# Picking a looked-up row by its high digit: a chain of conditional copies, or one masked product and one sum

## The chip, the cores and the metric

The kernel runs on one core of a Trainium2 chip. The metric is the device time of one execution in microseconds, the median over runs; the profile is of one execution.

## What is computed

A layer of a graph network: 12,500 nodes with 16 features, 400,000 edges with 64 attributes each and a weight; edges are sorted by destination.

```python
h = max(layernorm(x), 0)
h = h @ W_node.T                       # 12500 x 16
rf = edge_attr @ W_review.T            # 400000 x 16
m = (h[src] + rf) * edge_weight
out = x + segment_sum(m, dst, 12500)
```

The products with the weights are made after the sums: attributes and rows of h are summed by destination first, and the 96-row sum is multiplied by both weights at the end.

## The kernel before

**Two ways to fetch h[src].** The edges are cut into 25 blocks of 125 lists of 128 edges. For 10 blocks ("gathered") GpSimd fetches the rows of h by indirect DMA, 1250 transfers of 128 rows (L487), with 8 slots of 5 transfers in flight; it waits for the slot to be summed (summed_p). For the other 15 blocks ("sorted") the sources of each list were sorted at the start, so rank j of each of the 125 lists points near row 98 x j of the table. TensorE looks the rows up by a product with a 0/1 matrix.

**The lookup.** The table of h lies in SBUF as fp16 in two parts (top and rest), 98 chunks of 128 rows. A source is split in a low part (one of 512, the "hot" matrix, 4 columns of 128) and a high digit of up to 8 values. A list block is worked in STEPS = 16 steps of RANKS = 8 ranks. In a step, `look_up` (TensorE, 64 matmuls, L969) makes for each of the 8 ranks a product with WIDTH[x] candidates of 16 features, one for each value of the high digit, into PSUM tile found[x % 2]: 125 partitions (lists) x 8 ranks x WIDTH x 16. WIDTH is 4, 6, 7, 7, 7, 8 seven times, 7, 7, 6, 5: 112 in all. Then `choose` (VectorE) keeps the candidate of the right digit, in found_h[125, 128 ranks, 16]. The mask (uint8, one plane of 128 ranks per digit) is made once a list block by `mark` (L727).

**choose.** The first digit is a product found x mask (L737). Each further digit is a copy_predicated over the same 8 x 16 elements (L742), which waits for the semaphore `chosen` of the one before it. TensorE waits for the last one before it writes the same found again two steps later (L961), and before it turns found_h for the rest (turn_ranks, L974 to L977).

**The order of VectorE's work** is written out by hand. In step x of block u: choose(x - 1); two hot columns for a later step (make_hot, L702, 2004 fp16 each); add_step(x - 1), the adds of the previous sums into acc, each with a register load of its base from base_row (L763, L771) and a wait for the add before it (L767, L775); the 0/1 matrices that bring the rows of the block before back in the order of the edges (make_perm, L757); the hits of later groups (L746), for which ScalarE waits (L545). After step 15: choose(15), adds, then split_ranks (L784) after TensorE and ScalarE. TensorE in a step: look_up, unsort of the block before (L983), sums (L995, L1004). SP loads attributes and the rows of low parts. After 15 such blocks there is a last stretch of 16 steps without lookup, then the product with the weights and the output.

All of it runs in a loop over passes, of which this input needs one.

Of the kernel before, what the change touches and what calls it, by code (L numbers as in the profile page):

```python
# [13 lines left out]
P = 128  # L14
# [35 lines left out]
BEFORE = [sum(WIDTH[:x]) for x in range(STEPS + 1)]  # L50
ALL_WIDTHS = BEFORE[STEPS]

# [33 lines left out]
def bass_gnn_preln(  # L86
# [47 lines left out]
    with ExitStack() as ctx:  # L134
# [6 lines left out]
        acc = sb("acc", [FS, N + WINDOW])  # L141
# [12 lines left out]
        big = sb("big", [P, 2 * NA * HOT // 2 + P * H])  # L154
        hot = big[:, 0:NA * HOT].bitcast(F16).rearrange("p (k a n) -> p k a n", k=2, a=NA)
# [42 lines left out]
        back_row = sel_p[:, 0, 2:4, :].rearrange("p j w -> p (j w)")  # L198
        stat = sel_p[0:C, 1:3].rearrange("p s j w -> p (s j w)")[:, 0:4 * NP].rearrange("p (k i) -> p k i", k=4)
# [6 lines left out]
        start_row = sb("start_row", [P, P])  # L206
        top_row = sb("top_row", [P, P])
        limit = sb("limit", [P, P])
# [7 lines left out]
        base_row = sb("base_row", [1, NG], I32)  # L216
# [55 lines left out]
        found_in = sem("found_in")  # L272
        chosen = sem("chosen")
# [178 lines left out]
        def _(pool):  # L452
# [20 lines left out]
            nc.gpsimd.memset(acc[:], 0.0).then_inc(acc_step, 1)  # L473
# [125 lines left out]
        def _(dve):  # L599
# [60 lines left out]
            link(nc.vector.tensor_scalar(start_row[:], iota[:], 98.0 / 128.0, 49.0 / 128.0, ALU.mult, ALU.add))  # L660
            link(nc.vector.tensor_tensor(start_row[:], start_row[:], back_row, ALU.subtract))
            link(nc.vector.tensor_scalar(start_row[:], start_row[:], 0.0, 1.0 / 256.0 - 0.5, ALU.max, ALU.add))
            link(nc.vector.tensor_scalar(start_row[:], start_row[:], ROUNDER, None, ALU.add))
            link(nc.vector.tensor_scalar(start_row[:], start_row[:], ROUNDER, None, ALU.subtract))
            link(nc.vector.tensor_scalar(top_row[:], width_row[:], float(-NA), float(CHUNKS), ALU.mult, ALU.add))
            link(nc.vector.tensor_tensor(start_row[:], start_row[:], top_row[:], ALU.min))
            link(nc.vector.tensor_scalar(start_row[:], start_row[:], float(P), None, ALU.mult))

            dve.wait_ge(span_in, 16)
            nc.vector.tensor_copy(base_row[:], span_row[:, 0, :])  # L670
# [27 lines left out]
            nc.vector.tensor_scalar(limit[:], width_row[:], 2.0, None, ALU.subtract)  # L698
# [12 lines left out]
            with dve.Fori(0, end) as ps:  # L711
# [18 lines left out]
                def choose(u, x):  # L730
                    before = ps * (SORTED * ALL_WIDTHS) + u * ALL_WIDTHS + BEFORE[x]
                    dve.wait_ge(found_in, ps * (SORTED * STEPS) + u * STEPS + (x + 1))
                    if x == 0:
                        dve.wait_ge(mask_in, ps * SORTED + u + 1)
                    ranks = slice(x * RANKS, (x + 1) * RANKS)
                    of_digit = found[x % 2][0:C, :].rearrange("p (j b f) -> p b j f", j=RANKS, f=H)
                    nc.vector.tensor_tensor(found_h[:, ranks, :], of_digit[:, 0], mask[:, 0, ranks].unsqueeze(2).to_broadcast([C, RANKS, H]),  # L737
                                            ALU.mult).then_inc(chosen, 1)
                    for b in range(1, WIDTH[x]):
                        dve.wait_ge(chosen, before + b)  # L740
                        dve.sem_inc(begun_dve, 1)
                        nc.vector.copy_predicated(found_h[:, ranks, :], mask[:, b, ranks].unsqueeze(2).to_broadcast([C, RANKS, H]),  # L742
                                                  of_digit[:, b]).then_inc(chosen, 1)
# [51 lines left out]
                for step in range(STEPS):  # L795
                    if step:
                        choose(0, step - 1)
                    make_hot(0, step)
                    if step:
                        add_p(step - 1, step - 1, added + (step - 1))  # L800
# [288 lines left out]
```

## Time and profile before

| what | value |
|---|---|
| median of 3 runs | 2129.21 us (2125.23 to 2130.02) |
| profiled execution, time | 2126.73 us |
| profiled execution, span | 2124.9 us |
| mean granted TensorE clock | 0.863 of full |
| TensorE, VectorE, ScalarE, GpSimd busy | 78%, 74%, 42%, 68% |

The time includes what lies around the span from first to last instruction. Busy time is the union of an engine's instructions. "Idle before" is an engine's idle time just before a group of instructions, and behind the arrow what ended it; an idle time shorter than a certain size is counted but has no releaser named.

### The profile page before, as it was taken

The numbers are of one execution on the slowest core, as the hardware profiler recorded it, in microseconds if no ns is written. First come the engines' busy times: TensorE is split into PE (matmuls) and PEld (weight loads), VectorE is DVE, ScalarE is ACT, GpSimd is POOL, SyncE is SP. The second block draws the span as 40 slices with busy tenths as digits, with TensorE's granted clock in tenths as the row PEclk, the third lists the DMA queues.
The fourth block names the chain that finished last, engine by engine and source line by source line (L and its number), as shares of the span: only waits on it lengthen the run. The fifth ranks groups of instructions, "written<-read, shape, count | busy, mean of one in ns | idle before, by whom it ended". The sixth has DMA issues, their size and how long they took to land.

```text
span 2124.9 us, 75085 instructions
## 1 busy us (share of the span) xinstructions
PE 1650.7 (78%) x23874; PEld 1615.4 (76%) x23874; DVE 1575.2 (74%) x3975; ACT 895.3 (42%) x3561; POOL 1451.5 (68%) x1301
## 2 busy tenths in 40 slices
PE   1119887898878988887888879798887898878776
PEld 0018787888878888787888878788787888878765
DVE  5978777777777777777777777777777777777754
ACT  1212444444444444444544444444444444444452
POOL 2716777777767767676776767767676777767720
PEclk9559899988989899899988989889899989989855
DMA  3513344344444444444443444534444544434532
GB/s 116 80 39 88 75 98 104 81 98 98 87 98 94 96 99 86 97 99 86 98 93 84 102 89 86 114 80 86 105 90 87 103 88 97 99 80 106 100 52 44
DMA packets 512172, 191.43 MB, mean 90 GB/s; under 512 B 472234, under 2 KB 495359, under 8 KB 511479
## 3 DMA queue, kind: packets, MB, share of 16 engines
q1 hardware_dynamic: 469361, 173.64, 35.8%
q0 software_dynamic: 40000, 10.32, 5.0%
q8 instruction: 223, 3.65, 0.7%
q10 hardware_dynamic: 2368, 2.02, 0.4%
q14 instruction: 220, 1.80, 0.3%
HBM read 182.96 MB, written 2.89 MB: 87 GB/s over the span
## 4 chain that ended last, share of the span: by engine, by line
DVE 39%; issue 21%; DVEq 17%; PE 15%; ACT 4%; DMA 2%; SPq 1%; ACTq 1%
DVE big L742 15%; DVEq L771 7%; PE found L969 6%; DVE mid L746 5%; PE seg L1004 5%; DVEq L763 4%; DVE hit_p L746 4%; DVE perm L757 3%; ACT mid L545 3%; DVE big L702 2%; DVE big L737 2%; PE found L977 2%; DVE acc L775 1%; DMA w_rows<-in_L_gnn_W_node_dram 1%; PE seg L995 1%
## 5 line engine op out<-in xcount | busy, mean ns | idle before, releaser
L487 POOL DMA_INDIRECT vals_p<-h_ext,idx_t x1250 | 1436.5, 1149 | 586.2 <-issue 356.6
L969 PE MATMUL found<-table,big 128*128 128x128 f16 (+4 forms) x15360 | 891.5, 225 | 70.7 <-DVE by_rank L784 21.9
L969 PEld LDWEIGHTS found<-table,big 128*128 128x128 f16 x15360 | 871.4, 106 | 80.5 <-issue 79.9
L545 ACT ACTIVATE sel_p<-hit_p,wgt_t 128x64 f32<-128x64 f16 x1250 | 325.6, 336 | 1024.8 <-DVE hit_p L746 1022.4
L742 DVE COPY_PREDICATED big<-mask,found 125x128 f32<-125x128 uint8 x1440 | 434.3, 302 | 218.0 <-DVE big L742 15.6
L1004 PE MATMUL seg<-mid 128*96 128x64 f32 x3750 | 426.4, 277 | 210.6 <-ACT mid L558 210.4
L1004 PEld LDWEIGHTS seg<-mid 128*96 128x96 f32 x3750 | 401.4, 191 | 224.4 <-ACT mid L545 139.9
L545 ACT ACTIVATE mid<-mid,wgt_t 128x64 f32<-128x64 f16 x1875 | 467.9, 332 | 14.5 <-DVE mid L746 14.5
L702 DVE TENSOR_SCALAR big<-low_all,own 128x2004 f16<-128x2004 f16 x484 | 340.9, 747 | 11.9 <-DMA low_all<-low_dram 11.9
L775 DVE SCALAR_TENSOR_TENSOR acc<-seg,count_s,acc 96x64 f32 x375 | 105.0, 280 | 217.7 <-DVE acc L767 82.9
L995 PE MATMUL seg<-sel_p,vals_p 128*80 128x64 f32 x2500 | 235.2, 244 | 0.0
L995 PEld LDWEIGHTS seg<-sel_p,vals_p 128*80 128x80 f32 x2500 | 213.9, 160 | 0.1
L757 DVE TENSOR_TENSOR perm<-edge_no,pos_t 128x768 f16<-128x768 f16 x375 | 192.9, 546 | 0.0
L746 DVE TENSOR_TENSOR mid<-iota,rel_t 128x320 f16<-128x320 f32 x375 | 168.3, 480 | 0.0
L983 PE MATMUL edge_h<-by_rank,perm 128*128 128x32 f16 x1875 | 154.5, 241 | 8.1 <-DVE perm L757 5.6
L983 PEld LDWEIGHTS edge_h<-by_rank,perm 128*128 128x128 f16 x1875 | 126.4, 127 | 9.1 <-DVE perm L757 5.8
L746 DVE TENSOR_TENSOR hit_p<-iota,rel_t 128x320 f16<-128x320 f32 x250 | 119.8, 480 | 0.0
L767 DVE SCALAR_TENSOR_TENSOR acc<-seg,count_p,acc 80x64 f32 x250 | 68.2, 273 | 33.2 <-issue 31.6
L558 ACT COPY mid<-edge_h 128x160 f32<-128x160 f32 x375 | 88.7, 276 | 0.0
L977 PE MATMUL found<-ident,big 125*128 125x125 f32 x240 | 48.3, 386 | 49.8 <-DVE big L742 49.8
L977 PEld LDWEIGHTS found<-ident,big 125*128 125x128 f32 x240 | 43.9, 219 | 51.8 <-DVE big L742 51.8
L737 DVE TENSOR_TENSOR big<-found,mask 125x128 f32<-125x128 f32 x240 | 67.0, 279 | 0.2 <-PE found L969 0.2
(128 smaller groups left out, 316.1 us busy)
## 6 DMA issues: line engine op xcount, KB each, us to landing
low_all<-low_dram SPq DMA_DIRECT2D x120, 501.0 KB
mid<-in_edge_attr_dram SPq DMA_DIRECT2D x375, 160.0 KB
vals_p<-in_edge_attr_dram SPq DMA_DIRECT2D x250, 160.0 KB
vals_p<-h_ext,idx_t POOLq DMA_INDIRECT x1250
big<-in_src_dram SPq DMA_DIRECT2D x1, 1562.5 KB
big<-in_dst_dram SPq DMA_DIRECT2D x1, 1562.5 KB
big<-in_edge_weight_dram SPq DMA_DIRECT2D x1, 1562.5 KB
h_ext<-mid SPq DMA_DIRECT2D x2, 781.2 KB
```

The lines of the kernel that those rows point to most:

```text
L487: pool.indirect_dma_start(vals_p[:, q % RP, j, R:F], None, h_ext, bass.IndirectOffsetOnAxis(ap=idx_t[:, q * J + j:q * J + j + 1], axis=0), ...
L545: last = nc.scalar.activation(sel[:, j, :], hit[:, j, :], ACT.Copy, scale=wgt_t[:, bass.ds(tile + j, 1)])
L702: return nc.vector.tensor_scalar(hot[:, k, a, :], low_all[:, k, :], own[:, a:a + 1], None, ALU.is_equal)
L742: nc.vector.copy_predicated(found_h[:, ranks, :], mask[:, b, ranks].unsqueeze(2).to_broadcast([C, RANKS, H]), of_digit[:, b]).then_inc(cho ...
L746: return nc.vector.tensor_tensor(hit, iota[:, 0:WINDOW].unsqueeze(1).to_broadcast([P, J, WINDOW]), rel_t[:, bass.ds(tile, J)].unsqueeze(2) ...
L757: nc.vector.tensor_tensor(perm[:, g % RS], edge_no[:], pos_t[:, bass.ds(u, 1), g, :].to_broadcast([P, P, J + 1]), ALU.is_equal).then_inc(p ...
L771: base = dve.value_load(base_row[0:1, bass.ds(u * GROUPS + (NQ + g), 1)], min_val=0, max_val=N)
L969: last = nc.tensor.matmul(found[x % 2][:, r * P:r * P + n], hot[:, x // 2 % 2, a, col:col + P], rows, start=(a == 0 and part == 0), stop=( ...
L977: last = nc.tensor.transpose(found[i][:, f * P:f * P + C], found_h[:, :, i * HALF_F + f], ident[0:C, 0:C])
L983: last = nc.tensor.matmul(edge_of(g)[:, q * 2 * H:(q + 1) * 2 * H], perm[:, g % RS, :, q], by_rank[:, :, :, g * J + q].rearrange("p i f -> ...
L995: last = nc.tensor.matmul(seg_p(x), vals_p[:, slot, j, :], sel_p[:, x % RH, j, :], start=(j == 0), stop=(j == J - 1))
L1004: last = nc.tensor.matmul(seg_s(g), vals_s[:, g % RS, j, :], sel_s[:, g % RS, j, :], start=(j == 0), stop=(j == J - 1))
```

## The change

`choose` becomes two functions. `mask_found` multiplies all WIDTH[x] candidates of the 8 ranks with their masks in one instruction, into a new SBUF tile `masked` (125 x 8 x 8 x 16, fp32); `add_digits` sums over the digit with one tensor_reduce whose input is the view with the digit as inner axis, 16 elements apart. make_hot comes between the two. The semaphore `chosen` counts reductions, a new one `masked_in` counts products, and TensorE's look_up waits for `masked_in`.

```diff
-                def choose(u, x):
-                    before = ps * (SORTED * ALL_WIDTHS) + u * ALL_WIDTHS + BEFORE[x]
-                    dve.wait_ge(found_in, ps * (SORTED * STEPS) + u * STEPS + (x + 1))
+                def mask_found(u, x):
+
+                    before = ps * (SORTED * STEPS) + u * STEPS + x
+                    dve.wait_ge(found_in, before + 1)
                     if x == 0:
                         dve.wait_ge(mask_in, ps * SORTED + u + 1)
+                    dve.wait_ge(chosen, before)
                     ranks = slice(x * RANKS, (x + 1) * RANKS)
-                    of_digit = found[x % 2][0:C, :].rearrange("p (j b f) -> p b j f", j=RANKS, f=H)
-                    nc.vector.tensor_tensor(found_h[:, ranks, :], of_digit[:, 0], mask[:, 0, ranks].unsqueeze(2).to_broadcast([C, RANKS, H]),
-                                            ALU.mult).then_inc(chosen, 1)
-                    for b in range(1, WIDTH[x]):
-                        dve.wait_ge(chosen, before + b)
-                        dve.sem_inc(begun_dve, 1)
-                        nc.vector.copy_predicated(found_h[:, ranks, :], mask[:, b, ranks].unsqueeze(2).to_broadcast([C, RANKS, H]),
-                                                  of_digit[:, b]).then_inc(chosen, 1)
+                    of_digit = found[x % 2][0:C, :].rearrange("p (j b f) -> p j b f", j=RANKS, f=H)
+                    marks = mask[:, 0:WIDTH[x], ranks].rearrange("p b j -> p j b")
+                    nc.vector.tensor_tensor(masked[:, :, 0:WIDTH[x], :], of_digit[:, :, 0:WIDTH[x], :],
+                                            marks.unsqueeze(3).to_broadcast([C, RANKS, WIDTH[x], H]), ALU.mult).then_inc(masked_in, 1)
+
+                def add_digits(u, x):
+                    dve.wait_ge(masked_in, ps * (SORTED * STEPS) + u * STEPS + (x + 1))
+                    dve.sem_inc(begun_dve, 1)
+                    ranks = slice(x * RANKS, (x + 1) * RANKS)
+                    nc.vector.tensor_reduce(found_h[:, ranks, :], masked[:, :, 0:WIDTH[x], :].rearrange("p j b f -> p j f b"),
+                                            AX.X, ALU.add).then_inc(chosen, 1)
...
                     for step in range(STEPS):
                         if step:
-                            choose(u, step - 1)
+                            mask_found(u, step - 1)
                         make_hot(u, step)
+                        if step:
+                            add_digits(u, step - 1)
                         if step:
                             add_step(step - 1)
...
-                    choose(u, STEPS - 1)
+                    mask_found(u, STEPS - 1)
+                    add_digits(u, STEPS - 1)
                     add_step(STEPS - 1)
...
                     if x >= 2:
-                        pe.wait_ge(chosen, ps * (SORTED * ALL_WIDTHS) + u * ALL_WIDTHS + BEFORE[x - 1])
+                        pe.wait_ge(masked_in, ps * (SORTED * STEPS) + u * STEPS + (x - 1))
```

To make room in SBUF, `base_row` moves into row 96 of the buffer of acc (partition 96 in place of 0), `start_row` into a part of sel_p that is free at the start, and `limit` (width - 2) is folded into the constant of another instruction:

```diff
-        acc = sb("acc", [FS, N + WINDOW])
+        acc_raw = sb("acc", [P, N + WINDOW])
+        acc = acc_raw[0:FS, :]
+        base_row = acc_raw[FS:FS + 1, 0:NG].bitcast(I32)
...
+        masked = sb("masked", [C, RANKS, WIDEST, H])
...
-            nc.vector.tensor_scalar(limit[:], width_row[:], 2.0, None, ALU.subtract)
...
-                        after(nc.vector.tensor_scalar(turn[:, 5:6], turn[:, 6:7], -2000.0, None, ALU.mult))
-                        after(nc.vector.tensor_scalar(top_row[:], limit[:], turn[:, 5:6], None, ALU.add))
+                        after(nc.vector.tensor_scalar(turn[:, 5:6], turn[:, 6:7], -2000.0, -2.0, ALU.mult, ALU.add))
+                        after(nc.vector.tensor_scalar(top_row[:], width_row[:], turn[:, 5:6], None, ALU.add))
```

## Rows read from the trace of the kernel before

**Rows 1.** The page, part 1: busy time and share of each engine.
```profile
PE 1650.7 (78%) x23874; PEld 1615.4 (76%) x23874; DVE 1575.2 (74%) x3975; ACT 895.3 (42%) x3561; POOL 1451.5 (68%) x1301
```

**Rows 2.** L727 (min/median/max ns, first and last start); busy time between these two starts.
```profile
L727 DVE TENSOR_TENSOR mask<-digit_now,digit x15: 1214/1226/1298, 161.2 to 1892.1; 125x1024 uint8<-125x1024 f16 x15
...
161.20:1892.10 1730.90, 1453.19 (x21711) 1430.66 (x21709) 1303.68 (x3485) 768.38 (x3113) 1278.96 (x1120) 0.90 0.43 93
```

**Rows 3.** Waits of VectorE, 160 to 2010 us: total, times, longest.
```profile
DVE acc L775 <- PE seg L1004: 41.5, 76, 0.8
...
DVE big L737 <- PE found L969: 0.2, 1, 0.2
```

**Rows 4.** Instructions by line and form, VectorE: busy us, mean ns, idle before.
```profile
L742 DVE COPY_PREDICATED big<-mask,found 125x128 f32<-125x128 uint8 x1440 | 434.3, 302 | 218.0 <-DVE big L742 15.6 <-DVE big L737 1.9 <-issue 1.1
L702 DVE TENSOR_SCALAR big<-low_all,own 128x2004 f16<-128x2004 f16 x484 | 340.9, 747 | 11.9 <-DMA low_all<-low_dram 11.9
...
L775 DVE SCALAR_TENSOR_TENSOR acc<-seg,count_s,acc 96x64 f32 x375 | 105.0, 280 | 217.7 <-DVE acc L767 82.9 <-DVE acc L775 77.3 <-PE seg L1004 53.9
...
L737 DVE TENSOR_TENSOR big<-found,mask 125x128 f32<-125x128 f32 x240 | 67.0, 279 | 0.2 <-PE found L969 0.2
```

**Rows 5.** Timeline of VectorE around a step of width 7: start, us.
```profile
1016.92 1.49 DVE L702 TENSOR_SCALAR big<-low_all,own 128x2004 f16<-128x2004 f16 x2
...
1019.81 0.48 DVE L746 TENSOR_TENSOR hit_p<-iota,rel_t 128x320 f16<-128x320 f32 x1
1020.21 0.48 DVE L746 TENSOR_TENSOR mid<-iota,rel_t 128x320 f16<-128x320 f32 x1
1020.61 0.28 DVE L737 TENSOR_TENSOR big<-found,mask 125x128 f32<-125x128 f32 x1
1021.03 2.54 DVE L742 COPY_PREDICATED big<-mask,found 125x128 f32<-125x128 uint8 x6
1023.48 0.75 DVE L702 TENSOR_SCALAR big<-low_all,own 128x2004 f16<-128x2004 f16 x1
```

**Rows 6.** GpSimd, 165.7 to 2036.5 us: its gathers, its waits, its last gather.
```profile
L487 POOL DMA_INDIRECT vals_p<-h_ext,idx_t x1210 | 1387.0, 1146 | 533.3 <-issue 344.7 <-PE seg L995 188.6
...
POOL vals_p L487 <- PE seg L995: 188.6, 80, 47.5
...
2035.49 2.94 POOL L487 DMA_INDIRECT vals_p<-h_ext,idx_t  x1 [0.30 <-issue]
```

**Rows 7.** Rows from which an added instruction is priced: by form, timeline (sort), by source.
```profile
L784 DVE TENSOR_TENSOR by_rank<-found,by_rank 128x1000 f16<-128x1000 f32 x30 | 35.7, 1199 | 7.3 <-ACT by_rank L564 6.7
...
L625 DVE TENSOR_REDUCE span<-big 125x5 f32<-125x3200 f32 x1 | 3.5, 3489 | 0.0
...
L614 DVE TENSOR_REDUCE sel_p<-mid 125x100 f32<-125x1600 f32 x1 | 1.8, 1820 | 0.0
...
L505 ACT COPY wgt_t<-found 128x500 f32<-128x500 f32 x6 | 6.2, 1298 | 0.0
...
L505 ACT CAST idx_t<-found 128x500 int32<-128x500 f32 x2 | 1.1, 566 | 0.0
...
114.88 1.16 DVE L652 TENSOR_TENSOR big<-by_rank 125x960 f32<-125x960 f32 x1
115.95 1.20 DVE L653 TENSOR_TENSOR big<-by_rank 125x960 f32<-125x960 f32 x1
...
L977 PEld LDWEIGHTS found<-ident,big x240: 185/230/231, 240.7 to 2014.2; 125*128 125x128 f32 x120
...
L930 PEld LDWEIGHTS found<-ident,big x75: 137/226/231, 28.5 to 141.5; 125*128 125x128 f32 x75
...
L930 PEld LDWEIGHTS found<-ident,by_rank x15: 183/230/231, 127.3 to 130.1; 125*128 125x128 f32 x15
```

**Rows 8.** Timeline of VectorE in the last stretch: the add of gathered group 249.
```profile
2079.44 0.28 DVE L767 SCALAR_TENSOR_TENSOR acc<-seg,count_p,acc 80x64 f32 x1 [1.16 <-issue]
```

More of the change, by code:

```diff
@@ L49 @@
 START = [start_of(j) for j in range(P)]
-BEFORE = [sum(WIDTH[:x]) for x in range(STEPS + 1)]
-ALL_WIDTHS = BEFORE[STEPS]
 BLOCKS = STEPS // 2
@@ L198, in bass_gnn_preln @@
         back_row = sel_p[:, 0, 2:4, :].rearrange("p j w -> p (j w)")
+        start_row = sel_p[:, 3, 0:2, :].rearrange("p j w -> p (j w)")
         stat = sel_p[0:C, 1:3].rearrange("p s j w -> p (s j w)")[:, 0:4 * NP].rearrange("p (k i) -> p k i", k=4)
@@ L205, in bass_gnn_preln @@
         width_row = sb("width_row", [P, P])
-        start_row = sb("start_row", [P, P])
         top_row = sb("top_row", [P, P])
-        limit = sb("limit", [P, P])
         zeros = sb("zeros", [P, H])
@@ L215, in bass_gnn_preln @@
         span_row = low_all[0:1].rearrange("p k n -> p (k n)").bitcast(F32)[:, 0:2 * NG].rearrange("p (k g) -> p k g", k=2)
-        base_row = sb("base_row", [1, NG], I32)
         reach = sb("reach", [1, 4])
@@ L272, in bass_gnn_preln @@
         found_in = sem("found_in")
+        masked_in = sem("masked_in")
         chosen = sem("chosen")
@@ L472, in _ @@
             nc.gpsimd.memset(pos_t[:], 0.0).then_inc(made, 1)
-            nc.gpsimd.memset(acc[:], 0.0).then_inc(acc_step, 1)
+            nc.gpsimd.memset(acc, 0.0).then_inc(acc_step, 1)
             pool.wait_ge(h_stored, 16)
@@ L657, in _ @@
             assert here is key_a
[L660 to L664, printed above, removed]
+            link(nc.vector.tensor_scalar(start_row, iota[:], 98.0 / 128.0, 49.0 / 128.0, ALU.mult, ALU.add))
+            link(nc.vector.tensor_tensor(start_row, start_row, back_row, ALU.subtract))
+            link(nc.vector.tensor_scalar(start_row, start_row, 0.0, 1.0 / 256.0 - 0.5, ALU.max, ALU.add))
+            link(nc.vector.tensor_scalar(start_row, start_row, ROUNDER, None, ALU.add))
+            link(nc.vector.tensor_scalar(start_row, start_row, ROUNDER, None, ALU.subtract))
             link(nc.vector.tensor_scalar(top_row[:], width_row[:], float(-NA), float(CHUNKS), ALU.mult, ALU.add))
-            link(nc.vector.tensor_tensor(start_row[:], start_row[:], top_row[:], ALU.min))
-            link(nc.vector.tensor_scalar(start_row[:], start_row[:], float(P), None, ALU.mult))
+            link(nc.vector.tensor_tensor(start_row, start_row, top_row[:], ALU.min))
+            link(nc.vector.tensor_scalar(start_row, start_row, float(P), None, ALU.mult))
             dve.wait_ge(span_in, 16)
-            nc.vector.tensor_copy(base_row[:], span_row[:, 0, :])
+            nc.vector.tensor_copy(base_row, span_row[:, 0, :])
             link(nc.vector.tensor_reduce(reach[:, 0:1], span_row[:, 1, :], AX.X, ALU.max))
@@ L796, in _ @@
                     if step:
-                        choose(0, step - 1)
+                        mask_found(0, step - 1)
                     make_hot(0, step)
+                    if step:
+                        add_digits(0, step - 1)
                     if step:
@@ L807, in _ @@
                             hits_s(0, g)
-                choose(0, STEPS - 1)
+                mask_found(0, STEPS - 1)
+                add_digits(0, STEPS - 1)
                 add_p(STEPS - 1, STEPS - 1, added + (STEPS - 1))
@@ L826, in _ @@
                         if step:
-                            choose(u, step - 1)
+                            mask_found(u, step - 1)
                         make_hot(u, step)
+                        if step:
+                            add_digits(u, step - 1)
                         if step:
@@ L899, in _ @@
                 after(nc.vector.tensor_tensor(count_s[:], turn[:, 6:7], h_only[:], ALU.max))
-                after(nc.vector.tensor_scalar(base_row[:], base_row[:], turn[0:1, 3:4], float(N), ALU.add, ALU.min))
+                after(nc.vector.tensor_scalar(base_row, base_row, turn[FS:FS + 1, 3:4], float(N), ALU.add, ALU.min))
                 assert nxt[0] == NEXT, nxt
@@ L974, in turn_ranks @@
                     for i in range(2):
[L975 removed]
+                        pe.wait_ge(chosen, ps * (SORTED * STEPS) + u * STEPS + STEPS)
                         for f in range(HALF_F):
```

1 line of the change is left out of this document (removed).

## The prediction

> **What bounds the kernel now.** I read the page's busy shares first. TensorE is busy 78% of the span, VectorE 74%, GpSimd 68% [rows 1]: no engine is full, so shares alone decide nothing. The change touches only the loop over the fifteen sorted lists, and there one list lasts (1892.1 - 161.2)/14 = 123.6 us from mask to mask [rows 2]. In those 1730.9 us TensorE is busy 1453, VectorE 1304 and GpSimd 1279 [rows 2].
>
> The second view is the waits. The reader is to see who waits for whom. VectorE hardly ever waits for TensorE: 0.2 us before the first selection of a step and 41.5 us, spread over 76 waits, before an add into acc [rows 3]. What leaves VectorE "idle" is its own chain: the conditional copies are busy 434.3 us and idle 218.0 us before them [rows 4], one short gap per copy, because each waits for the semaphore of the one before it. The timeline shows it for a step of width 7: product at 1020.61, six copies from 1021.03, the next hot column at 1023.48, while independent instructions of 0.48 us follow each other 0.40 us apart [rows 5]. So VectorE works through its list of instructions with nothing outside it ending the waits: the loop is bound by VectorE, by latency and work together.
>
> Third, who comes next. GpSimd issues 1210 gathers after the first forty; each costs 1146 ns plus about 0.3 us, and of the 188.6 us that it waits for a free slot, 47.5 are the wait before the loop fills [rows 6]. The 80 waits in it carry the usual 0.3 us too, so about 188.6 - 47.5 - 24 = 117 us are slack. TensorE has 1731 - 1453 = 278 us idle in the fourteen periods [rows 2].
>
> **The change, part by part.** There are 15 x 16 = 240 steps, 112 digits a list, 7 on average, each of 128 elements. So a step handles 7 x 128 = 896 elements on average, 215,040 in all.
>
> Removed: 240 products (67.0 us) and 1440 copies (434.3 us), with 218.0 + 0.2 us of gaps [rows 4], 719.5 us. The next hot column starts some 0.08 us before the last copy ends, as independent instructions do [rows 5]: less 240 x 0.08 = 19. That is 700 us of VectorE's time. The step of rows 5 taken alone gives 2.87 x 240 = 689, which agrees within 2%.
>
> Added, first, one product over all digits, out of PSUM with a uint8 mask. The nearest rows are the product over 128 elements, 279 ns [rows 4], and a product out of PSUM over 1000 elements, 1199 ns [rows 7]: (1199 - 279)/872 = 1.055 ns an element. 896 elements take 279 + 768 x 1.055 = 1089 ns, x 240 = 261 us. The reading and the writing are in runs of 16 times the width, as contiguous as in those rows, so I allow this term only 3% either way.
>
> Added, second, one reduction over the digit. Contiguous reductions cost 1820 ns for 1600 elements and 3489 for 3200 [rows 7], so 1.043 ns an element and 151 fixed: 1086 ns for 896, x 240 = 261 us. But this one doesn't read contiguously. Its inner axis is the digit, so every element lies 16 words (64 bytes) behind the one before. No VectorE row reads like that, and here the whole forecast hangs. Below: 1.04, and nothing less, since no reduction of the trace beats it. The sort's last pair reads and writes every second word and takes 1.16 and 1.20 us for 960 elements [rows 7], so a step of two words costs nothing. Above: ScalarE's writes with a step of 25 words took 1298 ns for 500 elements, and 566 where the step was one [rows 7], so (1298 - 566)/500 = 1.46 ns an element for the step, together 2.50. Between them, TensorE reads the very tensor in question with a step of 16 words when it loads found_h as weights: median 230 ns for 128, against 226 to 230 for a contiguous block [rows 7]. SBUF gives words of this step at 230/128 = 1.8 ns a word without a loss. This is the nearest row (same step, same memory), and the middle of the two ends is 1.77; I take 1.75, estimated from these. The price of the step is then (1.75 - 1.04) x 215,040 = 153 us.
>
> The sum of the two: 261 + 261 = 522, less 480 x 0.08 = 38 where independent instructions overlap, plus 15 x 0.15 = 2 at the last step of each list, where the reduction stands right behind its product and waits for it as a copy does now: 486 us. Without the price of the step VectorE gets 700 - 486 = 214 us; with it 214 - 153 = 61 us. The gain is gone at 1.043 + 214/215,040 ns = 2.04 ns an element.
>
> The Trainium skill, Vector Engine (DVE) Microarchitecture Reference, section 5.2 on measured stream behaviour, speaks against this change: a port keeps its full rate only in runs of two or more adjacent words, one source that hops each element costs 1.73 ns a column, and steps of 24 words on both sources or on the output 2.50 to 2.51. By 1.73 the sum would gain 66 us, by 2.50 it would lose 99. The trace disagrees on its strictest form, since the sort's step of two words ran at 1.04 [rows 7], and agrees with 2.50 as ScalarE shows it.
>
> Moved: the two hot columns now stand between product and reduction, 1.4 us [rows 5], and hide the reduction's wait. They can wait for low_all; that happened once in the whole run, 11.9 us before the loop [rows 4]. Queued behind the reduction are the adds into acc, permutations and hits; ScalarE waits for the hits, but they come no later than the sum says. TensorE is released from found after the product, not after the last copy; it never was what VectorE waited for at that point (0.2 us [rows 3]), so I cost it at nothing. The new wait of the product for the previous step's reduction is covered by everything between two steps, several us. No DMA moves, so SP's and GpSimd's queues keep their order.
>
> base_row moves to partition 96. The 625 register loads from it have no row; the gap ahead of an add in which one could be seen is 217.7/375 = 0.58 us [rows 4], mostly the wait for the add before it. I take no change, and as the bound either way a tenth of that: 625 x 0.058 = 36 us. limit goes, a constant is folded in: 0.2 us.
>
> GpSimd: 61 us fit in its 117 us of slack, but waits meet unevenly, and I take off 5. The profiled execution had a span of 2124.9 us and a time of 2126.7; 2126.7 - 61 + 5 = 2071. The median of the runs is 2.5 us above it, 2129.2. I give 2071, rounded between the two.
>
> **The rivals.** *The step is free, and GpSimd becomes the bound.* For it: the reduction has one source and writes once for seven reads, and two-word steps are free. Then VectorE offers 214 us, but GpSimd can't follow: 165.7 + 1210 x (1.146 + 0.3) = 1915 for its last gather in place of 2036.5 (start of it 2035.49 [rows 6]), and behind that stand the steps from the add at 2079.44 on [rows 8], 45 us, and some 5 for the landing: 1965 at best. With waits met unevenly 1990, the range of the case 1965 to 2030.
>
> *The step costs as much as ScalarE's (slower).* At 2.50 ns an element the reduction takes 151 + 896 x 2.50 = 2391 ns, the price of the step is 1.46 x 215,040 = 314 us, and VectorE loses 314 - 214 = 100: 2229. It decides from 2.04 ns on, at VectorE's reduction. For it: the only strided row of an elementwise engine; against it: that row is a write, by another engine, at a step that isn't a power of two. A value of 2.1 to 2.2 would give 2142 to 2164.
>
> *It cancels.* From 2.02 to 2.06 ns an element the price, 210 to 218 us, eats the 214: 2125 to 2133. Twice the contiguous price, 2.09, would lie just beyond.
>
> *The chain doesn't shrink as said.* If VectorE's freed time only uncovered waits for TensorE before the adds, the 41.5 us of [rows 3] would grow. TensorE needs 1453/14 = 104 us a list and would have 119, so this takes little from the forecast and belongs to the free case rather.
>
> **How the numbers follow.** Forecast (1.4 to 1.95 ns an element, 2020 to 2115): 0.38. Free step: 0.24. Cancels: 0.06. Slower: 0.32. 0.2% is 4.3 us, about what a measurement of this kernel can tell from no change. Faster 0.60, same 0.06, slower 0.34, as half of the cancelling case falls on the slow side and a little of the rest on the same side. Cases of both signs hold most of the chance, so the range must reach to both: 1985 to 2235 leaves out the best of the free step and anything beyond ScalarE's price. The likeliest case's own range is 2020 to 2115.
>
> **What would show it.** In the profile after: the product near 1089 ns on average (1230 at width 8, 680 at width 4); the reduction near 151 + 896 x 1.75 = 1720 ns for my forecast, 1086 for the free step, 2391 for the slow one; no idle time before either except 15 short waits; a list of 119 to 120 us; GpSimd's waits for slots down from 188.6 to some 130. The forecast is wrong if the reduction is not between 1.4 and 1.95 ns an element, if the register loads show up as gaps ahead of the adds, or if the lists shorten by less than VectorE's own sum says.

## The result and the profile after

The change made the kernel slower by 36 us, 1.8%: 2163.6 us (median of 4, 2160.6 to 2172.0) against 2127.2 (median of 4), ratio 1.0179 with a 95% interval of 1.0145 to 1.0213. The profiled execution took 2163.99 us, its span was 2162.2. I had forecast 2071.

Part 1 of the page of the changed kernel, the counterpart of [rows 1]:

```profile
PE 1671.6 (77%) x23874; PEld 1638.4 (76%) x23874; DVE 1721.1 (80%) x2774; ACT 895.8 (41%) x3561; POOL 1639.2 (76%) x1301
```

GpSimd is busy 188 us longer, although it does the same 1301 instructions. The same page, part 4, the chain that ended last:

```profile
POOL 69%; issue 17%; DVE 5%; DMA 3%; PE 3%; POOLq 1%; DVEq 0%; ACT 0%; ACTq 0%; SPq 0%
```

and part 5, the gathers (busy, mean ns, idle before):

```profile
L488 POOL DMA_INDIRECT vals_p<-h_ext,idx_t x1250 | 1624.1, 1299 | 469.5 <-issue 376.4
```

By source line, the same gathers with first and last start:

```profile
L488 POOL DMA_INDIRECT vals_p<-h_ext,idx_t x1250: 940/946/3138, 56.7 to 2108.4; - x179
...
  PE seg L1006: 52.1, 14
```

The last gather starts at 2108.4, before at 2035.5 [rows 6]: 72.9 us later. From there to the end of the span it is 53.8 us, before 89.4: 35.6 less. The difference is the 37.3 us that the span grew by. GpSimd's waits for a free slot fell from 188.6 us to 52.1, which is nearly the one wait before the loop fills. So GpSimd is now the bound, and it became slower itself: 1299 ns a gather and not 1149 (all 1250), 188 us in all.

The instructions that the change added, by form, counterparts of [rows 4]:

```profile
L747 DVE TENSOR_REDUCE big<-masked 125x128 f32<-125x1024 f32 x105 | 197.1, 1878 | 0.0
L740 DVE TENSOR_TENSOR masked<-found,mask 125x1024 f32<-125x1024 f32 x105 | 127.6, 1215 | 7.6 <-PE found L980 7.5
...
L747 DVE TENSOR_REDUCE big<-masked 125x128 f32<-125x512 f32 x15 | 15.0, 1001 | 0.0
```

The reduction costs (1878 - 1001)/512 = 1.713 ns an element, the product 1215 ns for 1024. VectorE's two new instructions are what the forecast said. The loss is elsewhere.

The adds into acc, by form: those of sorted sums, the counterpart of L775 in [rows 4], and those of gathered sums, after and then before:

```profile
L780 DVE SCALAR_TENSOR_TENSOR acc<-seg,count_s,acc 96x64 f32 x375 | 105.2, 280 | 188.3 <-DVE acc L780 91.7 <-DVE acc L772 53.5 <-PE seg L1015 19.6
L772 DVE SCALAR_TENSOR_TENSOR acc<-seg,count_p,acc 80x64 f32 x250 | 68.4, 274 | 154.4 <-issue 153.8
```

```profile
L767 DVE SCALAR_TENSOR_TENSOR acc<-seg,count_p,acc 80x64 f32 x250 | 68.2, 273 | 33.2 <-issue 31.6
```

The idle time ahead of them grew from 250.9 us (217.7 and 33.2) to 342.7: 29 us less ahead of the sorted sums' adds, 121 more ahead of the gathered ones'. The profile names nothing that these waited for. With one gather of five, below, the 154 us are 21, so they go with the full number of gathers.

### The profile page after: what moved, and what is told of

The parts are those of the page before. It is cut to its first block, busy times and chain, and to the rows that moved or that the text cites. A ratio compares the mean times of both kernels' runs of the same rounds, so it can differ in the third digit from the quotient of the medians.

```text
span 2162.2 us, 71484 instructions
## 1 busy us (share of the span) xinstructions
PE 1671.6 (77%) x23874; PEld 1638.4 (76%) x23874; DVE 1721.1 (80%) x2774; ACT 895.8 (41%) x3561; POOL 1639.2 (76%) x1301
## 4 chain that ended last, share of the span: by engine, by line
POOL 69%; issue 17%; DVE 5%; DMA 3%; PE 3%; POOLq 1%; DVEq 0%; ACT 0%; ACTq 0%; SPq 0%
POOL vals_p L488 69%; DMA big<-in_dst_dram 2%; DMA vals_p<-h_ext,idx_t 1%; PE seg L1015 1%; PE found L980 1%; DVE by_rank L653 1%; DVE big L653 1%; DVE big L654 1%; DVE by_rank L654 1%; PE seg L1006 1%; POOLq L485 0%; DMA low_dram<-by_rank 0%; DVEq L776 0%; PE found L1070 0%; DMA low_all<-low_dram 0%
## 5 line engine op out<-in xcount | busy, mean ns | idle before, releaser
L488 POOL DMA_INDIRECT vals_p<-h_ext,idx_t x1250 | 1624.1, 1299 | 469.5 <-issue 376.4
L1015 PE MATMUL seg<-mid 128*96 128x64 f32 x3750 | 443.7, 284 | 43.3 <-ACT mid L559 43.0
L1015 PEld LDWEIGHTS seg<-mid 128*96 128x96 f32 x3750 | 422.3, 199 | 47.1 <-issue 33.2
L1006 PE MATMUL seg<-sel_p,vals_p 128*80 128x64 f32 x2500 | 255.8, 257 | 246.9 <-DMA vals_p<-h_ext,idx_t 238.1
L1006 PEld LDWEIGHTS seg<-sel_p,vals_p 128*80 128x80 f32 x2500 | 229.7, 171 | 262.3 <-issue 140.2
L747 DVE TENSOR_REDUCE big<-masked 125x128 f32<-125x896 f32 (+2 forms) x240 | 401.8, 1674 | 2.2 <-DVE masked L740 0.2
L740 DVE TENSOR_TENSOR masked<-found,mask 125x896 f32<-125x896 f32 (+2 forms) x240 | 259.5, 1081 | 20.1 <-PE found L980 19.7
L941 PE MATMUL found<-ident,big 125*128 125x125 f32 x75 | 14.4, 357 | 58.2 <-ACT big L499 28.6
L565 ACT CAST by_rank<-found 128x1000 f16<-128x1000 f32 x30 | 28.9, 992 | 70.8 <-PE found L988 70.8
```

Source lines behind the costliest of these rows:

```text
L488: pool.indirect_dma_start(vals_p[:, q % RP, j, R:F], None, h_ext, bass.IndirectOffsetOnAxis(ap=idx_t[:, q * J + j:q * J + j + 1], axis=0), ...
L740: nc.vector.tensor_tensor(masked[:, :, 0:WIDTH[x], :], of_digit[:, :, 0:WIDTH[x], :], marks.unsqueeze(3).to_broadcast([C, RANKS, WIDTH[x], ...
L747: nc.vector.tensor_reduce(found_h[:, ranks, :], masked[:, :, 0:WIDTH[x], :].rearrange("p j b f -> p j f b"), AX.X, ALU.add).then_inc(chose ...
L1006: last = nc.tensor.matmul(seg_p(x), vals_p[:, slot, j, :], sel_p[:, x % RH, j, :], start=(j == 0), stop=(j == J - 1))
L1015: last = nc.tensor.matmul(seg_s(g), vals_s[:, g % RS, j, :], sel_s[:, g % RS, j, :], start=(j == 0), stop=(j == J - 1))
```

## The experiments

The experiments were run in five sessions, and the kernel before was timed again in each. In three sessions it took 2127 us, in the other two 2738 and 2790. What that is stands at the end; the runs of those two sessions are told with the time of their own kernel before.

### Does the order decide, or the new instructions?

**sum_before_hot**, the reduction directly behind its product:

```diff
                             mask_found(u, step - 1)
-                        make_hot(u, step)
-                        if step:
                             add_digits(u, step - 1)
+                        make_hot(u, step)
```

> The changed kernel with the reduction directly behind its product, and the two hot columns behind it. Theory A (placement): GpSimd's gather is held while VectorE runs hot columns, permutations or hits, and what it costs depends on where in a gather these stretches fall. The stretch between the last hits and the first hot column goes back to about 2.9 us (product 1.0, wait 0.15, reduction 1.7), as in the kernel before, so the mean gather falls from 1301 ns to 1150 to 1180 and the time to 2100 to 2130 us, although VectorE pays 240 x 0.15 = 36 us of waits more. Theory B (the new instructions): the large product or the reduction hold the gather themselves; then the mean stays at 1300 ns or more and the time at 2160 to 2175 us.

**split_hot**, one hot column on each side of the reduction:

```diff
-                        make_hot(u, step)
+                        hot_half(u, step, 0)
                         if step:
                             add_digits(u, step - 1)
+                        hot_half(u, step, 1)
```

> The changed kernel with one hot column ahead of the reduction and one behind it, so that no two stand together. Theory A (placement): a gather that meets a hot column is held 0.7 us at most in place of 1.4, the mean gather falls below 1250 ns, and the time to 2090 to 2140 us. Theory B (the new instructions): mean gather and time stay as they are, 1300 ns and 2155 to 2165 us.

**chain_split**, the kernel before with its chain cut (part 0 is the product and two copies, part 1 the other copies):

```diff
-                            choose(u, step - 1)
+                            choose(u, step - 1, 0)
                         make_hot(u, step)
+                        if step:
+                            choose(u, step - 1, 1)
```

> The kernel before, its chain of copies cut in two: product and two copies, the two hot columns, the remaining copies. No instruction is added or removed. Theory A (placement): the stretch between hits and hot columns falls to 1.2 us, as in the changed kernel, so the mean gather rises from 1146 to 1250 to 1300 ns and the time to 2145 to 2170 us. Theory B (the new instructions): the mean gather stays near 1150 ns and the time within 5 us of the kernel before.

These three and contiguous_sum fell into the session with 2738 us. There sum_before_hot took 2666.9 (ratio 0.974), split_hot 2681.8 (0.981), chain_split 2731.8 (0.9975, interval 0.9947 to 1.0004). GpSimd had 640 us and more of waits for slots in each of them, so none could tell the theories apart. I ran the three again in another session, with the changed kernel among them.

> The changed kernel as it is, as a control beside the other runs of this call. On a chip where the kernel before takes 2127 us, 2160 to 2170 us with a mean gather of 1300 ns; on one where TensorE's issue binds and the kernel before takes 2738 us, about 2670 us, since GpSimd has slack there and VectorE's shorter chain shows.

> The reduction directly behind its product, run again beside the changed kernel itself. Theory A (placement): where GpSimd binds, the mean gather is 100 ns or more below that of the changed kernel and the time 30 to 60 us below it. Theory B (the new instructions hold the gathers): the same mean gather as the changed kernel, and a time at or above it.

> One hot column on each side of the reduction, run again beside the changed kernel. Theory A (placement): mean gather below 1250 ns and 20 to 70 us less than the changed kernel where GpSimd binds. Theory B: no difference beyond 5 us.

> The kernel before with the two hot columns after the product and two copies, run again on another call. Theory A (placement): on a chip where the kernel before takes 2127 us, the mean gather rises from 1146 ns to 1250 or more and the time to 2145 to 2170 us. Theory B: within 5 us of the kernel before.

Beside these four the kernel before took 2126.5 us:

| run | time us | ratio (95%) | mean gather ns, from 165.7 us |
|---|---|---|---|
| after_again | 2161.1 | 1.016 (1.014 to 1.018) | 1300 |
| sum_before_hot_2 | 2038.9 | 0.958 (0.956 to 0.960) | 1158 |
| split_hot_2 | 2095.3 | 0.986 (0.984 to 0.988) | 1244 |
| chain_split_2 | 2320.0 | 1.092 (1.090 to 1.093) | 1222 |

Moving the reduction ahead of the hot columns takes 122 us away, and the gathers are back near the 1146 ns of before. Theory A had the direction and the gather right; the time fell by far more than the 30 to 60 us that I had written. Product and reduction are unchanged in kind and number and, within 1% in all, in duration, so theory B is refuted. The traces refute it instruction by instruction too. In the changed kernel's, 246 gathers ran beside a reduction and none of the hot columns, hits and permutations: they took 943 ns on average and 953 at most. In that of sum_before_hot_2, 133 ran so beside a product: 946 on average, 962 at most.

What a gather takes beyond 0.945 us can be put down to the last hot column, hit or permutation that began while it ran. Worked out from the starts and durations in three traces, over the gathers from 165.7 us:

| trace | beyond 0.945 us, all gathers | at hot columns | at hits and permutations |
|---|---|---|---|
| before | 244 us | 57 us | 186 us |
| after | 431 us | 178 us | 250 us |
| sum_before_hot_2 | 258 us | 56 us | 201 us |

So 121 of the 188 us that the gathers gained come from the hot columns and 64 from hits and permutations, though the number of all these instructions is the same. How the order does it is seen in the timelines. The changed kernel, VectorE and GpSimd (start and duration, us):

```profile
1026.26 2.95 POOL L488 DMA_INDIRECT vals_p<-h_ext,idx_t  x1 [0.31 <-issue]
...
1027.52 0.88 DVE L751 TENSOR_TENSOR mid<-iota,rel_t 128x320 f16<-128x320 f32 x2
...
1028.32 0.94 DVE L740 TENSOR_TENSOR masked<-found,mask 125x768 f32<-125x768 f32 x1
...
1029.19 1.38 DVE L702 TENSOR_SCALAR big<-low_all,own 128x2004 f16<-128x2004 f16 x2
1029.52 1.86 POOL L488 DMA_INDIRECT vals_p<-h_ext,idx_t  x1 [0.30 <-issue]
1030.49 1.45 DVE L747 TENSOR_REDUCE big<-masked 125x128 f32<-125x768 f32 x1
```

The hot columns end at 1030.57, the gather that began in them at 1031.38, 0.81 us later: it is held until they end. Hits hold it too; the gather begun at 1026.26 ended at 1029.21, again 0.81 us behind the hits' end at 1028.40. So each held gather sets GpSimd's phase: the next one starts 0.3 us after, 1.1 us behind the hits. The product lasts about 1 us, and that next gather falls right into the start of the hot columns. In sum_before_hot_2:

```profile
1025.54 0.88 DVE L751 TENSOR_TENSOR mid<-iota,rel_t 128x320 f16<-128x320 f32 x2
...
1027.54 0.95 POOL L488 DMA_INDIRECT vals_p<-h_ext,idx_t  x1 [0.30 <-issue]
1027.71 1.86 DVE L747 TENSOR_REDUCE big<-masked 125x128 f32<-125x1024 f32 x1 [0.15 <-DVE masked L740]
1028.80 0.95 POOL L488 DMA_INDIRECT vals_p<-h_ext,idx_t  x1 [0.30 <-issue]
1029.49 1.40 DVE L702 TENSOR_SCALAR big<-low_all,own 128x2004 f16<-128x2004 f16 x2
1030.05 1.01 POOL L488 DMA_INDIRECT vals_p<-h_ext,idx_t  x1 [0.30 <-issue]
```

Two gathers run beside the reduction at 0.95 us each, unharmed, and the third comes so late into the hot columns that it loses 0.07. The Trainium skill, SBUF — State Buffer, section on the two separate sides, says that GpSimd takes a shared port pair in turns with VectorE's two-port instructions, and with those that have two inputs in SBUF if GpSimd's own reads SBUF, each for a whole instruction. The held gathers agree, with 0.8 us to finish behind the release; hits and permutations have two inputs in SBUF, and a gather is issued with idx_t, which lies there. That the phase shifts these holds is read from the timelines; the holds and the averages are measured over all gathers.

split_hot_2 fell within what theory A had said (1244 ns, 66 us less than the changed kernel). chain_split_2 met the rise of the gather only in part (1222 ns, I had said 1250 or more), and its time lies outside both theories. GpSimd had 293 us of slot waits, so gathers don't explain 193 us. A second cause was at work.

**contiguous_sum**:

```diff
-                    nc.vector.tensor_reduce(found_h[:, ranks, :], masked[:, :, 0:WIDTH[x], :].rearrange("p j b f -> p j f b"),
+                    nc.vector.tensor_reduce(found_h[:, ranks, :], masked[:, :, 0:WIDTH[x], :].rearrange("p j b f -> p j (b f)").rearrange("p j (f b) -> p j f b", b=WIDTH[x]),
```

> The changed kernel with the reduction over neighbouring elements (it leaves out the sum over digits and adds up neighbours in its place). The reduction should cost 151 + 896 x 1.043 = 1086 ns on average in place of 1674, 141 us less for VectorE. If GpSimd is the bound, the time falls by far less than 141 us: with a mean gather between 1250 and 1300 ns it is 2120 to 2160 us. If VectorE's sum still decided, it would be near 2025 us. A reduction that stays near 1.7 ns an element would mean that the step has no price and the reduction itself is slow.

This run belongs to the session with 2738 us too. It took 2593.4 us against 2738.1 (0.948, 0.943 to 0.952). Its reductions, by form:

```profile
L747 DVE TENSOR_REDUCE big<-masked 125x128 f32<-125x1024 f32 x105 | 127.2, 1211 | 0.0
L747 DVE TENSOR_REDUCE big<-masked 125x128 f32<-125x896 f32 x75 | 80.7, 1076 | 0.0
```

1211 ns in place of 1878: the step of 16 words is the price, 0.65 ns an element, and not the reduction as such. For the time the run says little, and its expected times don't apply: GpSimd waited 640 us for slots, and VectorE's products 206 us for lookups, so TensorE was the bound.

### What the change is worth to VectorE alone

```diff
-                    for j in range(J):
+                    for j in range(1):
                         pool.indirect_dma_start(
...
-                    pe.wait_ge(h_in[slot], ps * (in_pass * J * 16) + turn_of_slot * (J * 16) + J * 16)
+                    pe.wait_ge(h_in[slot], ps * (in_pass * 16) + turn_of_slot * 16 + 16)
```

> The changed kernel with one gather of the five per group (it leaves out four fifths of the rows of h for the gathered edges, which are zero), so that GpSimd can't bind. Theory A: GpSimd was the bound, and VectorE's own chain is what sum_before_hot_2 showed without the wait ahead of its reduction: 2039 - 34 = about 2005 us. Rival: the changed kernel is slow for a reason on VectorE or TensorE; then it stays near 2160 us.

> The kernel before with one gather of the five per group (the same part left out). It was bound by VectorE, so without the other gathers it stays within 10 us of 2127 us. The difference to after_one_gather is what the change is worth to VectorE alone: my sum said 61 us, and with the register loads of the adds hidden better about 120 us.

Measured: 1981.5 us (I had said about 2005) and 2123.1 us, in the same session. With GpSimd out of the way the change gains 141.6 us; the kernel before stays where it was. So GpSimd's bound turned a gain of 142 into a loss of 36. But 142 is more than twice the 61 of my sum. The adds, by form, before_one_gather:

```profile
L776 DVE SCALAR_TENSOR_TENSOR acc<-seg,count_s,acc 96x64 f32 x375 | 105.0, 280 | 221.0 <-DVE acc L768 85.2 <-DVE acc L776 75.4 <-PE seg L1005 55.6
L768 DVE SCALAR_TENSOR_TENSOR acc<-seg,count_p,acc 80x64 f32 x250 | 68.6, 274 | 33.2 <-issue 31.5
```

after_one_gather:

```profile
L781 DVE SCALAR_TENSOR_TENSOR acc<-seg,count_s,acc 96x64 f32 x375 | 104.9, 280 | 157.4 <-DVE acc L781 75.2 <-PE seg L1016 33.3 <-DVE acc L773 14.2
L773 DVE SCALAR_TENSOR_TENSOR acc<-seg,count_p,acc 80x64 f32 x250 | 68.4, 274 | 21.1 <-issue 21.1
```

The idle time ahead of the adds fell from 254.2 to 178.5 us, 75.7 us, on gaps for which I had taken no change.

### The register loads

Each add loads its base into a register of VectorE's queue. The theory: the queue can do that ahead of time only when no wait holds it. A chain of copies holds it until the last copy, two long instructions without waits don't. In chain_split the copies stand right ahead of the adds. The next run takes the base as the constant 0, which leaves out the load, the register instructions behind it and the window's address in a register:

```diff
-                    base = dve.value_load(base_row[0:1, bass.ds(q, 1)], min_val=0, max_val=N)
+                    base = 0
...
-                    window = acc[0:F, bass.ds(base, WINDOW)]
+                    window = acc[0:F, base:base + WINDOW]
```

> The kernel before with its chain of copies around the two hot columns (as chain_split), and the bases of the adds into acc taken as the constant 0 in place of a register load (it leaves out where the sums go). chain_split took 2320 us, with 0.9 us idle ahead of the first add of each step. Theory (register loads): the queue of VectorE can load a base only when it isn't held by a wait, and 0.9 us a step were the load behind the last copy; without loads the time falls by 190 us or more, to 2130 or below. Rival (the placement of the gathers, or TensorE's later sums, made chain_split slow): it stays above 2280 us.

This run fell into the session with 2790 us and took 2606.4 (0.934), which is above the rival's 2280. But both figures were meant for a kernel before of 2127 us, and here TensorE was the bound (GpSimd waited 636 us for slots): inconclusive. With one gather of five the kernel before took 2123.1 us even in the session with 2790, so I repeated the pair that way:

> The kernel before with its chain cut around the hot columns, and one gather of five per group (it leaves out four fifths of the rows of h for the gathered edges), so that neither GpSimd nor the slow issue of TensorE on some chips can matter. Theory (register loads): the copies that stand directly ahead of the adds hold VectorE's queue, so the load of the base is bare again: 2123 + 190 = about 2310 us, with about 0.9 us idle ahead of the first add of each step. Rival (the gathers made chain_split slow): about 2125 us.

> The same with the bases of the adds as the constant 0 in place of a register load (it also leaves out where the sums go). Theory (register loads): the 190 us go and some of the other gaps between adds too: 2000 to 2130 us. Rival (adds wait for TensorE, whatever the loads): above 2280 us.

Measured: 2320.5 us and 1920.2 us. The gathers had no part in chain_split's loss: it took 2320.0 with all of them. Without the loads and what belongs to them the time is 400 us less, twice the loss. The kernel before wasn't run without loads, so how much of the 400 it would gain itself isn't known. VectorE in chain_split_one_gather:

```profile
1007.61 2.07 DVE L746 COPY_PREDICATED big<-mask,found 125x128 f32<-125x128 uint8 x5
1010.58 0.28 DVE L771 SCALAR_TENSOR_TENSOR acc<-seg,count_p,acc 80x64 f32 x1 [0.90 <-PE seg L1012]
1011.87 0.28 DVE L779 SCALAR_TENSOR_TENSOR acc<-seg,count_s,acc 96x64 f32 x1 [1.01 <-DVE acc L771]
```

0.9 us stand bare ahead of the first add and up to 1.0 ahead of the next. What VectorE's queue did in the 0.9 us is recorded in the same trace: the last copy starts at 1009.38, behind its wait; a TENSOR_LOAD from base_row starts at 1009.67 and takes 0.30 us, register instructions follow, and the add starts at 1010.58. In the kernel before the load starts at 1017.26, while the hot columns of [rows 5] run. Without loads, by form:

```profile
L779 DVE SCALAR_TENSOR_TENSOR acc<-seg,count_s,acc 96x64 f32<-96x64 f32 x375 | 105.1, 280 | 26.1 <-PE seg L1012 12.9
L771 DVE SCALAR_TENSOR_TENSOR acc<-seg,count_p,acc 80x64 f32<-80x64 f32 x250 | 69.8, 279 | 40.4 <-PE seg L1012 18.7 <-issue 3.0 <-PE seg L1003 0.7
```

The gaps fell from 482 us (258.5 and 223.7) to 66.5. The profile had put them down to TensorE, to the add before and to "issue".

### Versions that might beat both

**perm_between**: the reduction ahead of the hot columns as in sum_before_hot, and the permutations between product and reduction. The edit against the changed kernel:

```diff
                             mask_found(u, step - 1)
+                        for g in groups_unsorted((step + 1) % STEPS):
+                            make_perm(t if step + 1 < STEPS else t + 1, g)
+                        if step:
                             add_digits(u, step - 1)
                         make_hot(u, step)
                         if step:
-                            add_digits(u, step - 1)
-                        if step:
                             add_step(step - 1)
-                        for g in groups_unsorted((step + 1) % STEPS):
-                            make_perm(t if step + 1 < STEPS else t + 1, g)
```

> The reduction directly ahead of the hot columns, but the permutations of the next step put between product and reduction. The wait ahead of the reduction (33.7 us in sum_before_hot_2) is covered, and permutations and hits no longer stand in one stretch. Expected 2039 - 30 = about 2010 us if VectorE still binds and the mean gather stays below 1200 ns; above 2039 us if the gathers fall worse again (mean over 1250 ns).

In the session with 2790 us it took 2764.6 (0.992). Again:

> The permutations between product and reduction, run again. Where the kernel before takes 2127 us: about 2010 us if the gathers fall well (mean below 1200 ns), above 2039 us if they fall badly (above 1250 ns). Where it takes 2740 to 2790 us: 1% faster at most, as before.

2009.9 us, ratio 0.945 (0.942 to 0.948), mean gather 1173 ns: what was expected for gathers that fall well. Of the reductions' 34 us of waits for their product, 6 are left.

**digits_inner**: sum_before_hot, and TensorE writes the candidates with the digit as inner axis; mask and masked are laid out alike. The line of the matmul:

```diff
...
-                                last = nc.tensor.matmul(found[x % 2][:, r * P:r * P + n], hot[:, x // 2 % 2, a, col:col + P], rows,
+                                last = nc.tensor.matmul(found[x % 2][:, r * P:(r + 1) * P].rearrange("p (f b) -> p b f", f=H)[:, 0:WIDTH[x], :], hot[:, x // 2 % 2, a, col:col + P], rows,
```

> The reduction directly behind its product, and TensorE writes its candidates with the digit as inner axis (each matmul's output has a step of 8 words in PSUM), so that product and reduction read and write neighbours. The reduction should fall from 1674 to about 1100 ns, the product stay near 1085. Theory: VectorE gains 240 x 0.58 = 139 us on sum_before_hot_2 (2039 us), GpSimd's gathers then bind at about 1930 for the last one, so 1960 to 1990 us. Rival: the stepped output slows TensorE's lookups (64 matmuls took 3.3 us for width 7), TensorE becomes the bound, and it is 2100 us or more.

2417.8 us, ratio 1.137 (1.134 to 1.140): the rival won. Its reduction fell to 1220 ns at width 8, but its lookups became slow, and the products waited 371 us for them. Matmuls of width 8 in digits_inner, then in perm_between_2:

```profile
L977 PE MATMUL found<-table,big 128*128 128x128 f16 x6720 | 750.7, 313 | 0.0
```

```profile
L979 PE MATMUL found<-table,big 128*128 128x128 f16 x6720 | 414.1, 225 | 12.8 <-DVE big L702 11.6
```

112 ns each in place of 62, by busy time, at a higher mean granted clock (0.95 against 0.875). The Trainium skill, SBUF — State Buffer, under Door 1: The DMA port swizzle, says that PSUM has lines of 8 bytes and that an access that isn't contiguous slows matmuls much; the rows agree.

**loads_first**: perm_between with the loads of a step ahead of its first add. **before_loads_first**: the same edit in the kernel before.

```diff
                     def add_step(x):
+                        first = base_p((t + 1) * STEPS + x)
+                        bases = [base_s(t, g) for g in SUMS[x]]
                         if SUMS[x]:
                             dve.wait_ge(summed_s, ps * NSG + t * GROUPS + SUMS[x][-1] + 1)
...
```

> perm_between with all bases of a step's adds loaded ahead of the first add's wait, in place of one load ahead of each add. Reduction and hot columns (about 3.1 us without a wait) should hide all of them; the idle time ahead of the adds, 182 us in perm_between_2, falls to about 100 and VectorE gains some 70 us. But GpSimd can start its last gather at 165.7 + 1210 x (1.173 + 0.30) = 1948 us at the earliest if its gathers fall as before, so the time falls by 5 to 30 us only, from 2010 to 1980 to 2005. If it falls by 70 us, GpSimd was not near its bound.

> The kernel before with all bases of a step's adds loaded ahead of the first add. Here only the two hot columns (1.4 us) can hide loads, since the copies ahead of them hold the queue. Three loads of 0.5 us or more each don't fit, so the gaps between adds shrink but one ahead of the first add appears: a gain of 20 to 60 us (2070 to 2105 us). If the loads weren't what stands in the gaps, no change.

loads_first took 1956.3 us, ratio 0.919 (0.917 to 0.921), the fastest here. I had said 1980 to 2005, with gathers of 1173 ns as the bound; they fell still better, 1133 ns, and GpSimd stays near its bound (6 us of waits for slots beside the one before the loop fills). before_loads_first took 2188.0, ratio 1.028 (1.026 to 1.030), slower where I had expected a gain. Its adds:

```profile
L783 DVE SCALAR_TENSOR_TENSOR acc<-seg,count_s,acc 96x64 f32 x375 | 105.2, 280 | 71.1 <-PE seg L1014 12.4 <-DVE acc L783 5.0 <-DVE acc L774 4.5
L774 DVE SCALAR_TENSOR_TENSOR acc<-seg,count_p,acc 80x64 f32 x250 | 69.9, 280 | 233.2 <-issue 133.3 <-PE seg L1014 80.4 <-PE seg L1005 19.6
```

Most of the gaps moved ahead of the first add, and together they grew from 250.9 us to 304.3. Behind a chain of waits there is only the 1.4 us of the hot columns to hide loads; behind the reduction there is twice that. In this trace the three loads of one step start at 1018.86, 1019.57 and 1020.30, one each 0.72 us, so three of them don't fit into 1.4.

## Why the prediction was wrong

**The masked product and the reduction: right.** 1081 ns on average against 1089, 1674 against 1720, 1.713 ns an element against 1.75. The Trainium skill's figure for one source that hops each element (1.73, Vector Engine (DVE) Microarchitecture Reference, section 5.2) was nearer still, though its row is for a hop of 4 KiB. That 1.75 came so close was partly luck. I had leaned on TensorE's 230 ns for 128 words with a step of 16, but TensorE takes 226 to 230 for neighbouring words as well [rows 7], so that row says nothing about what the step costs VectorE. The Trainium skill's strict form, that single words two apart are slow as well, stayed refuted by the sort [rows 7]. With the measured durations VectorE's sum is 700 - (259.5 + 401.8 - 38 + 2) = 75 us gained.

**The adds: wrong, a term left out.** I took "no change" for the gaps ahead of them, since the loads "have no row". With one gather of five they shrank by 76 us; 75 + 76 = 151, and the change measured 142 there. In the changed kernel itself, with all its gathers, they grew by 92 us. And the loads did have rows. The trace of before, by tile base_row, has

```profile
L771 DVEq TENSOR_LOAD <-base_row x375: 297/303/319, 260.2 to 2106.4; - x188
L763 DVEq TENSOR_LOAD <-base_row x250: 299/306/549, 165.7 to 2078.6; - x125
```

and part 4 of its page gives the queue a share of the chain that ended last:

```profile
DVE 39%; issue 21%; DVEq 17%; PE 15%; ACT 4%; DMA 2%; SPq 1%; ACTq 1%
```

**GpSimd: the step that failed.** "61 us fit in its 117 us of slack" kept the gather at 1.146 us, and the moved hot columns were priced for VectorE alone. I had counted what VectorE's instructions last, not where they fall in a gather. The new order brought the hot columns close behind the hits, the gather rose to 1.30 us, and 1210 x 0.155 = 188 us ate the 117 of slack and 71 more. The last gather came 73 us later; a shorter tail behind it gave 36 back. My rival "GpSimd becomes the bound" had the right engine, but with a fixed price and on the fast side. The rival that ended slower had the wrong engine.

**The range** (1985 to 2235) held the time, by the wrong mechanism. The sign and the likeliest case's own range (2020 to 2115) were wrong. That the slow rival's sum for 2.1 to 2.2 ns an element gives 2142 to 2164 is chance: the element cost 1.713.

**What would have shown it** was in the trace of before and not in my rows: [rows 6] have the mean gather alone, 1146 ns, and one long one of 2.94 us. The timeline of both engines together, of before, shows which instructions hold a gather:

```profile
1026.07 0.94 POOL L487 DMA_INDIRECT vals_p<-h_ext,idx_t  x1 [0.30 <-PE seg L995]
...
1027.32 2.35 POOL L487 DMA_INDIRECT vals_p<-h_ext,idx_t  x1 [0.30 <-issue]
1027.56 0.48 DVE L746 TENSOR_TENSOR hit_p<-iota,rel_t 128x320 f16<-128x320 f32 x1
1027.96 0.88 DVE L746 TENSOR_TENSOR mid<-iota,rel_t 128x320 f16<-128x320 f32 x2
```

The hits end at 1028.84, the held gather 0.83 us later; the one ahead of them took 0.94.

## What to carry to other kernels

When an engine's order changes, read again the price of every engine that shares a port with it: here moving one instruction ahead of two others was worth 122 us, by way of GpSimd, without changing any of them. And a chain of waits costs more than its gaps. It also holds the queue, so register loads behind it lie bare, and the queue's own rows (DVEq) show them; put long instructions without waits ahead of work that needs a register, and only then group the loads.

## What was not expected of the hardware

**Register loads.** A load into VectorE's queue takes 0.30 us, and with its register instructions the queue is taken for 0.72 us (before_loads_first). Where nothing hides it an add starts 0.9 us after the load (chain_split_one_gather), and the profile names TensorE, the add before or "issue" as what was waited for. Taking 625 of them away, with what belongs to them, was worth 400 us in chain_split.

**Two sessions with a slower TensorE.** There the kernel before took 29% and 31% longer, and TensorE was idle between the matmuls of one lookup. Waits of sum_before_hot in such a session:

```profile
PE found L978 <- issue: 372.5, 713, 1.2
```

In sum_before_hot_2, the same kernel, these waits come to 16.4 us, 14 times. The mean granted clock is 0.783 in sum_before_hot and 0.868 in sum_before_hot_2; what lowered it isn't shown. In the session where the kernel before took 2790 us, before_one_gather took 2123.1, so the slowness needs the full number of gathers. It isn't tied to one chip: the chip of that session gave 2126.7 us in a later one. Its cause stays open.
